# A macaron block (feed-forward, attention, feed-forward) on one core: weight test split in two, last tile in column halves, reciprocals in quarters

## The reference

```python
x = x + 0.5 * ffn(layernorm(x))
x = x + attn(layernorm(x))
x = x + 0.5 * ffn(layernorm(x))

def ffn(x):       # weights w are -1, 0 or 1 with a scale s per output; 128 -> 512 -> 512 -> 512 -> 128
    h = silu(x @ w1.T * s1) * (x @ w2.T * s2)
    h = gelu(h @ h1.T * sh1)
    h = gelu(h @ h2.T * sh2)
    return h @ w3.T * s3

def attn(x):      # h is a second layer norm of x, with gamma and beta
    keys, values = h @ Wk.T + bk, h @ Wv.T + bv
    weight = exp((keys @ Wka.T + bka) / sqrt(128))
    weight = weight / cumsum(weight, axis=tokens)
    return cumsum(weight * keys, axis=tokens) * values
```

## Time and profile before

| What | Before |
|---|---|
| median of 3 runs | 395.91 us |
| the profiled execution: own time | 396.45 us |
| the profiled execution: span | 394.7 us |
| PE busy | 382.2 us, 97% |
| PEld busy | 292.7 us, 74% |
| DVE busy | 337.2 us, 85% |
| ACT busy | 304.7 us, 77% |
| POOL busy | 49.9 us, 13% |
| outputs, x8 of 256 KB | 2.0 us from issue to landing |
| both waits of PE at the flag | 0.8 and 1.0 us |

### The profile page before, as it was taken

One profiled execution on the slowest core, in us unless ns is written; L12 is line 12 of the kernel. 1 busy time (PEld: TensorE's weight loads), 2 busy tenths in 40 slices (PEclk: granted clock), 3 DMA queues, 4 the chain that ended last, 5 costly groups with the idle time before them and its releaser, 6 DMA issues.

```text
span 394.7 us, 5879 instructions
## 1 busy us (share of the span) xinstructions
PE 382.2 (97%) x1670; PEld 292.7 (74%) x1670; DVE 337.2 (85%) x755; ACT 304.7 (77%) x513; POOL 49.9 (13%) x70
## 2 busy tenths in 40 slices
PE   7789999999999999999999999999999999999995
PEld 2367888777777787777687787777777777778883
DVE  4868778989989899998999899799899989976733
ACT  2767778996896799679779986877898778686763
POOL 4721011110100220101022010100411010020000
PEclk9999999999999999999999999999999999999999
DMA  7700000000000000000000000000000000000001
GB/s 265 261 1 2 0 2 0 1 0 2 0 2 0 0 0 0 0 0 0 0 0 0 0 0 27 0 0 27 0 0 27 0 27 0 27 2 0 27 2 55
DMA packets 3901, 7.45 MB, mean 19 GB/s; under 512 B 560, under 2 KB 1200, under 8 KB 3760
## 3 DMA queue, kind: packets, MB, share of 16 engines
q1 hardware_dynamic: 3168, 6.36, 4.5%
q10 hardware_dynamic: 720, 0.93, 0.7%
HBM read 5.19 MB, written 2.10 MB: 18 GB/s over the span
## 4 chain that ended last, share of the span: by engine, by line
PE 79%; DVE 11%; issue 4%; ACT 4%; POOL 0%; DVEq 0%; ACTq 0%; POOLq 0%
PE hid_ps L385 52%; PE gate_ps L385 6%; PE up_ps L385 5%; PE y_ps L385 5%; DVE rcsum L783 3%; PE y_ps L397 3%; PE xt_ps L397 2%; PE y_ps L521 2%; PE xt_ps L505 2%; DVE gate L700 1%; DVE csum L778 1%; ACT L632 1%; DVE full L710 1%; ACT full L572 1%; PE xt_ps L508 1%
## 5 line engine op out<-in xcount | busy, mean ns | idle before, releaser
L385 PE MATMUL hid_ps<-act_hi,hi_h 128*128 128x512 f32 x512 | 208.9, 408 | 1.0 <-DVE flag_i L661 1.0
L385 PE MATMUL hid_ps<-act_lo,hi_h 128*128 128x512 f32 x512 | 200.1, 391 | 0.0
L719 DVE TENSOR_TENSOR act_lo<-full,act_hi 128x512 fp32r<-128x512 f32 x189 | 124.2, 686 | 27.5 <-ACT act_hi L577 21.9
L572 ACT ACTIVATE full<-hid_ps,vec 128x512 f32<-128x512 f32 x128 | 88.0, 688 | 43.3 <-PE hid_ps L385 38.9
L385 PEld LDWEIGHTS hid_ps<-act_hi,hi_h 128*128 128x128 f32 x512 | 96.2, 188 | 25.3 <-issue 4.9
L385 PEld LDWEIGHTS hid_ps<-act_lo,hi_h 128*128 128x128 f32 x512 | 96.2, 188 | 23.0 <-issue 3.8
L577 ACT ACTIVATE act_hi<-full 128x512 fp32r<-128x512 f32 x128 | 79.4, 629 | 6.6 <-POOL nmr L287 5.3
L285 POOL TENSOR_TENSOR rstd<-veps,half 128x4 f32<-128x4 f32 x24 | 32.0, 1334 | 294.4 <-DVE veps L680 294.4
L710 DVE SCALAR_TENSOR_TENSOR full<-up_ps,s_half,gate 128x512 f32<-128x512 f32 x63 | 47.1, 748 | 1.5
L555 ACT ACTIVATE tanh<-gate_ps,s_half 128x512 f32<-128x512 f32 x63 | 42.4, 683 | 7.5 <-PE gate_ps L385 6.1
L560 ACT ACTIVATE act_hi<-full 128x512 fp32r<-128x512 f32 x64 | 40.2, 627 | 6.7 <-DVE full L710 6.4
(11 more groups left out here) (80 smaller groups left out, 347.9 us busy)
## 6 DMA issues: line engine op xcount, KB each, us to landing
out<-x_sb SPq DMA_DIRECT2D x8, 256.0 KB, 2.0
x_sb<-x SPq DMA_DIRECT2D x1, 1536.0 KB, 6.5
raw_h<-h2t SPq DMA_DIRECT2D x4, 256.0 KB, 6.9
raw_h<-h1t SPq DMA_DIRECT2D x2, 256.0 KB, 5.3
raw_h<-h1t ACTq DMA_DIRECT2D x2, 256.0 KB, 6.7
raw_w<-w2t ACTq DMA_DIRECT2D x1, 256.0 KB, 4.5
raw_w<-w1t SPq DMA_DIRECT2D x1, 256.0 KB, 4.3
x_sb<-x SPq DMA_DIRECT2D x1, 256.0 KB, 6.7
```

What stands on the lines that cost most here:

```text
L385: mm = eng.matmul(ps, w, a, start=(first and n == 0), stop=(last and n == len(seq_) - 1))
L572: eng.activation(full23[m % 2][:, :], hid_ps[m % 2][:, :], ACT.Gelu, scale=col("sh1" if n == 2 else "sh2", m)).then_inc(s_gelu[n], 1)
L719: eng.tensor_tensor(act_lo[n][:, m, :], full[m % 2][:, :], act_hi[n][:, m, :].bitcast(F32), ALU.subtract).then_inc(s_lo[n], 1)
```

## The change

1. The test of the weights is split. The first flag covers w1, w2 and h1, the second h2 and w3. PE takes the first branch ahead of `p2` of tile 0, and the second after `p2` of tile 0 and three chunks of `p1` of tile 1 (`SECOND_LAYER`). Because tile 1's first layer now starts before tile 0's second has ended, it gets activation buffers of its own (`act1_hi_second`). The programs of PE are now three: fast and fast, fast and plain, plain.
2. The stages at the start are reordered on all engines; POOL's casts wait for tile 0's `z`, and its `norm` of tile 1 comes ahead of its low parts; the transfer of tile 1's x comes one place earlier; seven warm-up matmuls (4, then 2, then 1, with waits for the layer norm of tile 0 between them) take the place of ten.
3. The end of the last step is done in two halves of 256 columns, in separate PSUM banks, with the last chunk of `p4` as one plain fp32 matmul per half, without `high` and `low`. The last output transfer becomes two of 128 KB.
4. `recip` (one per 256 columns before) becomes four of 128 columns. In the loop's third step on DVE three of the four now stand ahead of `xn_lo` and one behind it, and `up.0` and `values` each move ahead of a neighbour.

```diff
-WARM_UP = 10
+WARM_UP = (4, 2, 1)
     "PE": (
-        "t p1.0 p1.1 p1.2 p1.3 flag:sum",
+        "t p1.0 p1.1 p1.2 flag:sum1 p1.3",
...
+SECOND_LAYER = "p2a.0 p2a.1 t p2b.0 p2b.1 p2c.0 p2c.1 p1.0 p2d.0 p2d.1 p2.2 p1.1 flag:sum2 p2.3 p1.2"
 FIRST_STEP = {
-    "PE": "p2a.0 p2a.1 p2b.0 p2b.1 p2.2 p2.3 t p1.0 p1.1 p3.0 p1.2 p3.1 p1.3 p3.2 p3.3",
+    "PE": "p1.3 p3.0 p3.1 p3.2 p3.3",
...
-        "low3.1 a:recip.0 low3.2 low3.3",
-        "t a:recip.1 a:weight b:norm gate.0 low2.0 a:weight_keys up.0 low2.1 a:pool a:values gate.1 low2.2 "
+        "low3.1 a:recip.0 a:recip.1 low3.2 low3.3",
+        "t a:recip.2 a:recip.3 a:weight b:norm gate.0 low2.0 a:weight_keys up.0 low2.1 a:pool a:values gate.1 low2.2 "
...
-        "norm low1.2 low3.3 low1.3 b:cumsum b:recip.0",
-        "b:recip.1 low2.0 t b:weight low2.1 b:weight_keys gate.0 b:pool dt up.0 gate.1 b:values low2.2 up.1 "
+        "norm low1.2 low3.3 low1.3 b:cumsum b:recip.0 b:recip.1",
+        "b:recip.2 low2.0 t b:recip.3 b:weight low2.1 b:weight_keys gate.0 b:pool up.0 dt b:values gate.1 low2.2 up.1 "
...
+LAST_STEP = {
+    "PE": "p2.0 p2.1 p2.2 p2.3 p4 p3.0 p3.1 p3.2 dt last:p4a last:p3.0 last:p3.1 last:p4b last:p4c.0 last:p4c.1 "
+          "last:dt.0 last:dt.1",
+    "ACT": "gelu2.0 gelu2.1 high2.0 high2.1 gelu2.2 high2.2 gelu2.3 high2.3 gelu3.0 p4 high3.0 gelu3.1 high3.1 gelu3.2 "
+           "high3.2 last:gelu.0 last:gelu.1 last:delta",
+    "DVE": "low2.0 low2.1 low2.2 low2.3 low3.0 low3.1 dt low3.2 last:delta last:dt.0 last:dt.1",
...
+        last_hid = [halves(hid_ps[1], 0), halves(gate_ps[0], 1)]
+        last_y = [halves(gate_ps[1], 0), halves(xt_ps, 1)]
+        last_dt = [halves(up_ps[0], 0), halves(up_ps[1], 1)]
...
             norm(0)
+            eng.wait_ge(s_z, 1)
             for k in range(MC):
                 hi("h1", k)
             hi("w1", 0)
             hi("w2", 0)
-            hi("h2", 0)
+            norm(1)
             for m in range(POOL_FIRST):
                 low1(m)
-                hi("h2", m + 1)
-            norm(1)
+            for k in range(MC):
+                hi("h2", k)
...
+            def last_p4_end(h):
+                eng.wait_ge(s_last_gelu, h + 1)
+                eng.matmul(last_y[h], wblk(raw, "w3", MC - 1, 0), halves(full23[(MC - 1) % 2], h), start=False,
+                           stop=True).then_inc(s_last_p4, 1)
...
+            warm_up(WARM_UP[0])
+            eng.wait_ge(s_ve, 1)
+            warm_up(WARM_UP[1])
+            eng.wait_ge(s_pow, 1)
+            warm_up(WARM_UP[2])
...
                 with eng.If_eq(flag, 0):
-                    schedule("PE", stages(False, 1, [(s_xhi, 1), (s_xlo, 1)]), False)
+                    schedule("PE", stages(False, 1, [(s_xhi, 1), (s_xlo, 1)]), "second")
+                    eng.wait_ge(s_flag, 2)
+                    eng.reg_load(flag, flag_i[0:1, 1:2])
+                    with eng.If_eq(flag, 0):
+                        schedule("PE", stages(False, 2, [(s_xlo, 2)]), "rest")
+                    with eng.Else():
+                        schedule("PE", stages(True, 2, [(s_xlo, 2)]), "rest")
                 with eng.Else():
...
                 elif stage == "att_recip":
                     eng.wait_ge(s_cs, t + 1)
-                    b = batches()[chunk]
+                    b = slice(chunk * P, (chunk + 1) * P)
                     eng.reciprocal(rcsum[:, b], csum[:, b]).then_inc(s_rc, 1)
```

More of the change, by code:

```diff
@@ L37 @@
         "stats aggr veps bits:w1 norm",
-        "bits:w2 vec:scales t bits:h1.0 bits:h1.1 bits:h1.2 gate.0 up.0 gate.1 up.1 bits:h2.2 gate.2 up.2 bits:w3 "
-        "flag:raise flag:copy gate.3 up.3 low1.3 stats aggr veps",
+        "bits:w2 t vec:scales bits:h1.0 stats gate.0 up.0 aggr veps gate.1 flag:raise1 up.1 flag:copy1 "
+        "gate.2 norm up.2 gate.3 up.3 1:t low1.3",
     ),
 }
+SECOND_LAYER = "p2a.0 p2a.1 t p2b.0 p2b.1 p2c.0 p2c.1 p1.0 p2d.0 p2d.1 p2.2 p1.1 flag:sum2 p2.3 p1.2"
 FIRST_STEP = {
[3 rows of a table removed]
+    "PE": "p1.3 p3.0 p3.1 p3.2 p3.3",
+    "ACT": "bits:h2.0 bits:h2.1 tanh.0 gelu2.0 high2.0 gelu2.1 high2.1 high1.0 tanh.1 gelu2.2 high2.2 high1.1 gelu2.3 "
+           "tanh.2 high2.3 tanh.3 high1.2 gelu3.0 high3.0 high1.3 gelu3.1 high3.1 zwait z gelu3.2 high3.2 gelu3.3 "
            "high3.3",
[2 rows of a table removed]
+    "DVE": "bits:h2.2 bits:h2.3 gate.0 up.0 bits:w3 flag:raise2 low2.0 low2.1 flag:copy2 low1.0 gate.1 up.1 "
+           "low2.2 low1.1 gate.2 low2.3 up.2 gate.3 stats up.3 low1.2 aggr veps low3.0 low1.3 low3.1 norm low3.2 low3.3",
 }
@@ L210, in macaron_block, with first_act @@
             sem(n) for n in ("s_cs", "s_rc", "s_wg", "s_wgk", "s_pool", "s_adelta", "s_at", "s_x2"))
+        def first_act(T):
+            return "second" if isinstance(T, int) and T == 1 else 1
         def act_z(t):
@@ L266, in _ @@
                               x_sb[:, bass.ds(t * TOK + NT * TOK, TOK)]).then_inc(s_out, 16)
-            eng.wait_ge(s_out, 16 * NT)
+            for h in range(2):
+                eng.wait_ge(s_last_x, h + 1)
+                eng.dma_start(halves(out[:, (NT - 1) * TOK:], h),
+                              halves(x_sb[:, (2 * NT - 1) * TOK:], h)).then_inc(s_out, 16)
+            eng.wait_ge(s_out, 16 * (NT + 1))
         @block.gpsimd
@@ L327, in step @@
                         emit(which, chunk, stage, L)
+                    elif which == "last":
+                        emit("last_" + stage, chunk, 2 * NT - 1, L)
                     elif which.isdigit():
@@ L347, in schedule @@
                     step(GROUP * L + (FIRST + s), orders[s], L)
-            for i in range(2 * NT - 2, 2 * NT + 1):
-                step(i, orders[GROUP], None)
+            step(2 * NT - 2, orders[GROUP], None)
+            step(2 * NT - 1, LAST_STEP[engine], None)
         class Uses:
@@ L518, in _, with warm_up @@
             eng.wait_ge(s_const, 4)
[L520 to L523 removed]
+            def warm_up(n):
+                for _ in range(n):
+                    eng.matmul(y_ps[0:1, 0:seq], ones[:, 0:1], ones[:, :], start=True, stop=True)
+            warm_up(WARM_UP[0])
[3 more added lines that the diff above has]
+            warm_up(WARM_UP[2])
+            schedule("PE", stages(False, 0, []), "start")
             with eng.register("flag") as flag:
@@ L612, in emit @@
                     high23(int(stage[-1]), t, chunk)
+                elif stage == "last_gelu":
+                    last_gelu(t, chunk)
+                elif stage == "last_delta":
+                    eng.wait_ge(s_last_p4, 1)
+                    eng.activation(halves(delta, 0), last_y[0], ACT.Copy,
+                                   scale=s3_half[:, 0:1]).then_inc(s_last_delta[0], 1)
                 elif stage == "p4":
@@ L770, in emit @@
                     low(int(stage[-1]), t, chunk)
+                elif stage == "last_delta":
+                    eng.wait_ge(s_last_p4, 2)
+                    eng.tensor_scalar(halves(delta, 1), last_y[1], s3_half[:, 0:1], None,
+                                      ALU.mult).then_inc(s_last_delta[1], 1)
+                elif stage == "last_dt":
+                    eng.wait_ge(s_last_dt, chunk + 1)
+                    xt = halves(x_sb[:, (2 * NT - 1) * TOK:], chunk)
+                    eng.tensor_tensor(xt, xt, last_dt[chunk], ALU.add).then_inc(s_last_x, 1)
                 elif stage == "dt":
```

132 lines of the change are left out of this document (93 added, 39 removed), and 4 rows, old and new, of the table FIRST_STEP.

## The result

| What | Before | After |
|---|---|---|
| median of 10 runs on one chip | 395.96 us | 396.56 us |
| profiled execution: own time | 396.45 us | 396.20 us |
| profiled execution: span | 394.7 us | 394.4 us |
| PE / DVE / ACT busy | 382.2 / 337.2 / 304.7 us | 382.7 / 337.9 / 304.6 us |

The ratio is 1.0023, with a 95% interval from 1.0013 to 1.0034: a little slower, but within the 0.3% that the prediction counts as no change, and 3.2 us above the forecast of 393.4. The two profiled executions differ by 0.3 us the other way, so they serve to place gains and losses, not to weigh half a microsecond. The kernel before has a spread that goes with the clock: of 25 executions measured beside the first experiments, the ten with a mean granted clock of 0.992 to 0.994 took 395.6 to 396.3 us and 13 of the others (0.996 to 0.998) 394.0 to 395.0, while the changed kernel's ten all have 0.997 or more.

A forecast was written before the change was run, and what follows sets the result against it. PE was taken as the bound in the loop, with waits to win at the start and end. Terms -4.5 + 2.6 - 0.6 = -2.5 gave 393.95 from the profiled 396.45, or 393.4 allowing for the median; range 390.6 to 395.8.

The forecast's parts named there:

- from the second layer to the next step: Start of the kernel: 17.1 + 18.6 + 0.2 + 0.9, so the next step at 36.8 instead of 41.26.
- the forecast's 4.5 us: Start of the kernel: the gain of the whole new start, 4.5 us, with bounds 2.7 and 5.4.
- the loop's term: Loop: the last quarter makes everything behind it 0.65 us later, 4 x 0.65 = 2.6 us lost, bounds 0 and 3.5.
- The reads of the flag: PE's sequencer at the start: the second flag load and second branch cost nothing, because the sequencer works ahead.
- B: Rival, PE's flag reads at the start: they are not hidden and cost two of 0.84, 395.1 us; chance 0.15.
- D: Rival, first layer: PE's clock rises too late after the shorter warm-up, up to 6.9 us, 400.3 us; chance 0.08.
- C: Rival, last chunk: halves of 256 columns cost the length of a load, 2.0 us more, 395.4 us; chance 0.07.
- The warm-up: Start of the kernel: seven warm-up matmuls end near 8.3, moving all of the first layer 1.2 us ahead.
- The end: Last step: output 1.0 us earlier, but PE's jump starts only 0.5 to 0.6 earlier, so a gain of 0.6.
- Rival A: Loop: it costs nothing, as `low2.3` and `veps` are covered after all, 390.8 us; chance 0.22.

The follow-up runs named there:

- the exchange: The changed kernel with `gelu3.2` ahead of `z` and its wait on ScalarE in the first step: 395.36 us, ratio 0.9999 against the kernel before.

## Why the prediction was wrong

**The step that failed** is the one from the second layer to the next step. I took 18.6 us of work, 0.2 for the sum and 0.9 of waits, and had the next step at 36.8. It came at 38.35. The first matmul of step 1 needs a bank that `gelu3.2` frees, and I had followed ACT's order only up to `gelu2.0`. Behind that, ACT waits in order at `zwait z` for a layer norm that the new order on DVE had made 2.5 us later (`veps` at 34.80, not 32.28), while the rest had moved 4 us ahead; the 5.3 us of slack there had been were gone. That is 1.33 of the forecast's 4.5 us, shown by the exchange, which gives 1.2 to 1.3 back by the profile and 0.95 by the medians.

The work of step 0 did end where I had it (36.79 starts its last matmul), but by luck. The second layer began at 15.73, 1.4 ahead of my 17.1, and from there to the end of the step it took 21.3 us, where I had 19.7. I had no wait at its third matmul. There is one, 0.72 before 17.48: `up.2` on DVE stood behind a `z` that took 1.65 beside POOL's low parts. The two errors cancel.

**The size of the loop's term** was the other half: 2.6 forecast, 3.3 measured, 0.80 a pass. Of the mechanism most was there: idle in front of `xn_lo` (0.37; I had 0.5), a late `low2.3` (PE loses 0.38), a lag handed on through `veps`. The lag is what was mis-sized. The quarter that stands alone takes 0.97 from start to start, where three in a row take 0.85 each and I had 0.84, so DVE is 0.78 later from `wgt` on (4.42 us from the first reciprocal to `wgt` before, 5.20 now) and still 0.8 at `veps`; I had 0.65. I also left out `up.0`: I moved everything behind the quarter and then looked at `adelta` and `low2.3` only. PE's `p1.2`, ahead of `low2.3`, waits for `full` and loses 0.36. But that isn't what makes the pass longer: in the run with `dt` ahead of `up.0` PE waits 0.78 at that one place, and the pass is as long. By these runs a pass follows `veps`.

**What held.** The reads of the flag: 0.49 and 0.31 us on the sequencer, none before an idle PE, so B was wrong. The clock: the first two groups of the first layer start 0.93 apart (8.88, 9.81), as before (10.75, 11.68), D was wrong. The halves start 0.12 apart, so C was wrong:

```profile
386.32 0.28 PE L424 MATMUL hid_ps<-act_hi,hi_h 128*128 128x256 f32 x1
386.44 0.28 PE L424 MATMUL hid_ps<-act_lo,hi_h 128*128 128x256 f32 x1
```

The warm-up held in its direction only: I forecast 1.2 for the first layer and it was 1.9, since the 14 records took 5.17 us, not 6.0. All of it reached the second layer, of which I had kept 0.8 at `gate.0`. The end: 0.6 forecast, 0.7 in the profiled pair and 0.1 to 0.4 where only the end was changed. My reason for that number was incomplete: I had the jump and the output as two things that end together, and the jump lengthens the output.

**What I called cover.** Rival A put 0.22 on "the lag is only 0.65 and DVE stands still for 8 us in 128". Those 8 us are not behind the lag and in front of PE's next need; PE's margins were what counted: 0.3 at `low2.3`, which the earlier trace rows show, 0.1 at `up.0` (over at 123.55, wanted at 123.63), and none at the transposition behind `veps`.

In sum: -4.5 + 2.6 - 0.6 forecast, -2.9 + 3.3 - 0.7 in the profiled pair. The medians say 0.9 us more than that pair. Two things that differ between executions of the kernel before are each large enough for that: the spread with the clock (about 1.2 us between its two groups) and POOL's power, long or short for 0.36 us a pass. The profiled one had a clock of 0.999 and four long powers; how the ten behind the median divide is not on record.

## What to carry to other kernels

When one stage moves ahead by microseconds, follow each in-order queue through the stage behind it up to its next wait: the first instruction queued behind a wait for something that did not move ahead too, or that the new order has even moved back, can be the new bound. Here exchanging the two gave back 1.2 us. When an operation is put behind a wait to fill its idle time, count it in full against every consumer behind it, not only the one that was named. On an engine at 93% beside one at 99%, a removed stall in front bought nothing here, as the margins behind were 0.1 to 0.3 us.
